# Another order at the two ends of an attention and feed-forward kernel on one core

## The reference

```
x = x + layernorm(attention(layernorm(x)))      # x: 8 sequences x 512 tokens x 256
x = x + layernorm(ffn(layernorm(x)))

attention: q, k, v = complex projections of x (16 heads x 64)
  s    = Re(rot(q) . conj(rot(k)))
  maha = max(|q|^2 + E^2 |k|^2 - 2 E s, 0) / V   # E, V: functions of |i - j|, one pair of tables per head
  logits = coef * log1p(maha / nu) - 32 * log V, causal
  y = softmax(logits) v ; output = [Re y, Im y] @ Wo
ffn: silu(x Wg^T) * (x Wu^T) @ Wd^T              # hidden 768, weights int32 / 127
```

## Time and profile before

| | us |
|---|---|
| median of 3 runs (lowest, highest) | 1871.65 (1870.67, 1872.46) |
| the profiled execution, its time | 1871.72 |
| its span | 1869.9 |
| PE busy | 1795.5 |
| DVE busy | 1631.4 |
| ACT busy | 1576.7 |
| POOL busy | 1470.0 |

### The profile page before, as it was taken

How to read it: one execution, slowest core, us unless ns; L and a number is a source line. 1 busy time by engine, 2 the same in 40 slices (tenths; PEclk the granted TensorE clock), 3 DMA queues, 4 the chain that set the end, 5 groups by cost and what they waited for, 6 DMA issues and landing times.

```text
span 1869.9 us, 35435 instructions
## 1 busy us (share of the span) xinstructions
PE 1795.5 (96%) x10690; PEld 1475.9 (79%) x10690; DVE 1631.4 (87%) x3852; ACT 1576.7 (84%) x3255; POOL 1470.0 (79%) x1291
## 2 busy tenths in 40 slices
PE   5799999999999999999999999999999999988997
PEld 3577788878888888778888888788888888867876
DVE  7799989989888899988898899888898888986885
ACT  5798888898888888998888888988888888876654
POOL 5677888878888888888888888888888888862664
PEclk9899999999999999999999999999999999999999
DMA  6311211131112201131203111120112111010111
GB/s 184 118 68 46 85 46 68 45 104 46 63 52 68 86 26 67 46 125 46 68 30 101 46 63 52 63 98 33 69 46 91 46 46 45 25 57 13 46 46 45
DMA packets 61100, 117.77 MB, mean 63 GB/s; under 512 B 13504, under 2 KB 42944, under 8 KB 52720
## 3 DMA queue, kind: packets, MB, share of 16 engines
q1 hardware_dynamic: 60528, 115.51, 18.4%
q10 hardware_dynamic: 384, 0.00, 0.0%
HBM read 99.64 MB, written 21.36 MB: 65 GB/s over the span
## 4 chain that ended last, share of the span: by engine, by line
PE 70%; DVE 11%; ACT 4%; issue 3%; POOL 2%; DMA 0%; DVEq 0%; POOLq 0%; ACTq 0%; SPq 0%
PE pa L767 15%; PE py L831 13%; PE ps L807 12%; PE po L842 10%; PE pp L797 8%; PE pp L819 6%; PE pa L778 3%; PE pa L786 2%; DVE lg L1639 2%; DVE stats L1666 1%; DVE rm L1508 1%; DVE lg L1632 1%; DVE acc L1688 1%; DVE ps L1622 1%; DVE tabs L1753 1%
## 5 line engine op out<-in xcount | busy, mean ns | idle before, releaser
L592 POOL TENSOR_TENSOR qk<-rm 64x512 f32<-64x512 f32 x504 | 697.4, 1384 | 93.7 <-PE ps L807 49.8
L602 POOL TENSOR_TENSOR ek<-tabs,kn 128x512 f32<-128x512 f32 (+3 forms) x512 | 463.7, 911 | 133.9 <-DVE lg L1632 107.0
L1639 DVE CUSTOM_DVE_ANT_0 lg<-lg,tabs,ncog 128x512 f32<-128x512 f32 (+3 forms) x512 | 445.5, 888 | 0.0
L767 PE MATMUL pa<-xt,wt 128*128 128x512 f32 x1488 | 420.8, 418 | 6.3 <-DVE rm L1514 3.7
L1508 DVE TENSOR_TENSOR rm<-pa,tabs 128x512 f32<-128x512 f32 x504 | 327.0, 676 | 75.1 <-POOL qk L592 66.1
L807 PE MATMUL ps<-qk 128*128 128x512 f32 (+3 forms) x1024 | 366.9, 443 | 12.0 <-DVE lg L1632 11.8
L831 PE MATMUL py<-pt,vt 128*128 128x128 f32 x2560 | 348.2, 275 | 0.8 <-ACT pt L1214 0.5
L1632 DVE CUSTOM_DVE_ANT_0 lg<-ps,ek,qb 128x512 f32<-128x512 f32 (+3 forms) x512 | 279.0, 545 | 76.1 <-issue 58.0
L831 PEld LDWEIGHTS py<-pt,vt 128*128 128x128 f32 x2560 | 331.1, 192 | 16.8 <-ACT pt L1214 0.7
L767 PEld LDWEIGHTS pa<-xt,wt 128*128 128x128 f32 x1488 | 273.5, 191 | 58.7 <-issue 7.9
L1199 ACT ACTIVATE lg<-lg,qb 128x512 f32<-128x512 f32 (+3 forms) x512 | 273.0, 557 | 17.4 <-DVE lg L1632 13.5
(11 more groups left out here) (205 smaller groups left out, 2251.5 us busy)
## 6 DMA issues: line engine op xcount, KB each, us to landing
xt<-xs_d SPq DMA_DIRECT2D x56, 1024.0 KB, 4.8
tabs<-vec_d SPq DMA_DIRECT2D x7, 1536.0 KB, 6.5
xs_d<-xt SPq DMA_DIRECT2D x6, 1024.0 KB, 4.3
wt<-wraw_d SPq DMA_DIRECT2D x7, 768.0 KB, 6.7
acc<-in_L_attn_x SPq DMA_DIRECT2D x8, 512.0 KB, 6.2
tabs<-in_L_attn_x SPq DMA_DIRECT2D x8, 512.0 KB, 4.8
tabs<-rope_d SPq DMA_DIRECT2D x56, 64.0 KB, 5.8
out<-tabs SPq DMA_DIRECT2D x7, 512.0 KB, 3.2
```

The source lines that it names most:

```text
L592: pool.tensor_tensor(qk[part * DH:(part + 1) * DH, z * HH + hh, :], rm[row, 2 * part, :], rm[row, 2 * part + 1, :], ALU.add if part else A ...
L602: pool.tensor_tensor(ek[:, n % 2, 0:w], tab(par, hh, E2_T, w), kn[:, hh, 0:w], ALU.mult).then_inc(ek_pool, 1)
L767: last = mm(pa[r][:, :], wproj(par, z, kt, a, r * P, (r + 1) * P), xbuf[x][:, kt, b, :], start=(n == 0), stop=(n == 3 * KT - 1))
L1639: dve.tensor_tensor_reduce(lg[:, hh, at(n)], lg[:, hh, at(n)], tab(par, hh, T3_T, w), ncog[:, par, 0, hh:hh + 1], 3e38, ALU.add, ALU.min, ...
```

## The change

SP: the wait for the last logits and decay products of the group before the last, with `f_load(0)` and `f_load(1)` behind it, moves from behind the loop into iteration 57 (group 7, second sequence). TensorE: `down` waits for five low parts, and for the sixth in front of the sixth part's first product; weight transposes 0 and 1 move into the first iteration's body; in the preparation `x_turn(1)` goes behind `first_norms_k`, with three fillers in place of two; in the last body `turn(c, 0, 1)` and `gate_up(0, 0)` go ahead of the last output product, and `gate_up(0, 1)` goes into the run-out. ScalarE: copies 0 and 1 of the weights move into the first body, and all three rounds go ahead of `log(c, 0, 2)`; three exponentials go ahead of four copies in the run-out; `x_normal(1)` goes behind the two logarithms and `x_high(1)` behind `keep_norm_k`. VectorE and GpSimd: the statistics, the move and the power of sequence 1 go further back, the statistics of sequence 2 behind V_TABLES, and the four first rotations stand together.

```diff
 SP   for t in range(G * B - 2):
             g, j = divmod(t, B)
+            if j == 1 and g == G - 1:
+                sp.wait_ge(f_dve, 8 * B * (G - 1) + 8)
+                sp.wait_ge(ek_pool, 8 * B * (G - 1) + 8)
+                f_load(0)
+                f_load(1)
...
-        sp.wait_ge(f_dve, 8 * B * (G - 1) + 8)
-        sp.wait_ge(ek_pool, 8 * B * (G - 1) + 8)
-        f_load(0)
-        f_load(1)
         for b in range(2, B):
 POOL
-        x_rstd(1)
         pool.wait_ge(w_lo, 2 * KT)
-        pool.wait_ge(x_root, 2)
         first_rotated(0, 0, 0)
         first_rotated(0, 1, 0)
+        x_rstd(1)
+        pool.wait_ge(x_root, 2)
 PE   def down(b, half):
             if half == 0:
-                pe.wait_ge(f_hl, b * FT + FT)
+                pe.wait_ge(f_hl, b * FT + FT - 1)
...
                 for r in range(FT):
+                    if half == 0 and jj == 0 and r == FT - 1:
+                        pe.wait_ge(f_hl, b * FT + FT)
 PE   body
             if it.own == 1:
+                ffn_turn(0)
+                ffn_turn(1)
                 ffn_turn(2)
...
+            if not nxt:
+                turn(c, 0, 1)
+                gate_up(0, 0)
             if old:
                 out_project(cp, it.before, 1, 1)
-            turn(c, 0, 1)
-            if nxt:
+            if nxt:
+                turn(c, 0, 1)
                 scores(cn, 0, 2)
-            else:
-                gate_up(0, 0)
-                gate_up(0, 1)
 PE   preparation
         project(c0, 0, 0, 0, 0, 0, 1, 1)
+        keep_busy(3)
+        first_norms_k()
         x_turn(c0, 1, 0)
         x_turn(c0, 1, 1)
-        keep_busy(2)
-        first_norms_k()
...
-        ffn_turn(0)
-        ffn_turn(1)
 PE   run-out
         turn(c, 1, 2)
+        gate_up(0, 1)
         attend(c, 1, 0, 1)
 ACT  body
                 square(cn, 0, 0)
+            if it.own == 1:
+                ffn_keep(0)
+                ffn_keep(1)
+                ffn_keep(2)
+                ffn_cast_of(1)
             log(c, 0, 2, it.slot)
...
-            if it.own == 1:
-                ffn_keep(2)
-                ffn_cast_of(1)
 ACT  preparation
         first_high(2)
-        x_normal(1)
         square(c0, 1, 0)
         square(c0, 1, 1)
...
-        x_high(1, 0)
-        x_high(1, 1)
+        x_normal(1)
         act.wait_ge(ncog_dve, 1)
         keep_norm_k(c0, 0, 0)
         keep_norm_k(c0, 0, 1)
+        x_high(1, 0)
+        x_high(1, 1)
...
         ffn_cast_of(0)
-        ffn_keep(0)
-        ffn_keep(1)
 ACT  run-out
         keep_turned(c, 0, 1)
+        exp(c, 1, 1)
+        exp(c, 1, 2)
+        exp(c, 1, 3)
         keep_turned(c, 0, 2)
         keep_turned(c, 0, 3)
-        exp(c, 1, 1)
         keep_turned(c, 1, 0)
-        exp(c, 1, 2)
+        keep_turned(c, 1, 1)
         keep_y(c, 0)
-        keep_turned(c, 1, 1)
-        exp(c, 1, 3)
         keep_turned(c, 1, 2)
 DVE  preparation
         angle_clamp(-1)
-        x_stats(1)
...
         first_rotate(0, RS)
+        first_rotate(0, IS)
+        first_rotate(0, IC)
         step(tt(v_e2, v_e, v_e, ALU.mult))
         step(ts(v_e, v_e, -2.0, None, ALU.mult))
-        first_rotate(0, IS)
-        first_rotate(0, IC)
-        x_move(1)
+        x_stats(1)
         first_rotate(1, RC)
...
         first_rotate(1, IC)
+        x_move(1)
         start(0, 0)
-        x_stats(2)
...
         assert done[0] == V_TABLES, done
+        x_stats(2)
```

More of the change, by code:

```diff
@@ L485, in refill, with f_load @@
                 load_decay(g, par)
+            def f_load(b):
+                sp.dma_start(f_xin[b % 2], x_d[b].rearrange("(j p) n -> p j n", p=P)).then_inc(f_x[b % 2], 16)
             for t in range(G * B - 2):
@@ L517, in _ @@
                     load_rope(g + 1, (g + 1) % 2)
-            def f_load(b):
-                sp.dma_start(f_xin[b % 2], x_d[b].rearrange("(j p) n -> p j n", p=P)).then_inc(f_x[b % 2], 16)
             def f_store(b):
```

## The result

| | before | after |
|---|---|---|
| median, us | 1871.7 (20 runs, 1868.95 to 1873.21) | 1868.0 (20 runs, 1867.07 to 1869.32) |
| the profiled execution, its time and span | 1871.72, 1869.9 | 1869.32, 1867.5 |

The ratio after to before is 0.9982, 95% interval 0.9976 to 0.9989: 3.7 us faster, where 6.3 were forecast. The profiled executions differ by 2.4 us; the one of after is the slowest of its 20 runs.

A forecast was written before the change was run, and what follows sets the result against it. TensorE was taken to bound the long middle (396.8 of 400 us), so time could be won only outside it. Gains of 3.8 + 0.2 + 0.1 + 2.2 = 6.3 us from 1871.7 gave 1865.4 us, range 1862.3 to 1868.8.

The forecast's parts named there:

- rival C: Preparation gains nothing net, from low clock and weight turns in the first iteration's path; 1867.6, up to 1868.5 us; chance 0.17.
- the two signs that I had named for being wrong: Forecast wrong if the feed-forward's period falls by over 0.3 us, or the middle's first value product doesn't come earlier.
- rival E: Third iteration from the end: VectorE's own operations hold TensorE nearly as long; loads give 1.0, total 1868.5 us; chance 0.06.
- Part 1, loads: Third iteration from the end: earlier residual loads win 2.5 us idle time and 1.3 low clock, 3.8; least 2.5, most 4.3.
- That iteration at 26 to 26.6 us: Third iteration from the end, 30.02 us before, was to take 26 to 26.6 us once the loads came early.
- Part 2, sixth part: Feed-forward: the 1.01 us idle before down moves one product on, the period stays; gain 0.2 us, bounds 0 and 5.3.
- The ring over ScalarE's normalization and silu: Feed-forward: VectorE's loop through ScalarE's normalization, copy and silu sets the 18.94 us period, with no matmul late in it.
- Part 3, run-out: Run-out: 0.5 us lost and 0.6 won up to out_project(0,0), chain behind unchanged; gain 0.1 us, bounds +1.3 and -1.6.
- Part 4, preparation: Preparation: 0.9 us won up to the first weight cast, 1.7 behind it, less for clock; 2.2 us, bounds 4.5 and -6.6.
- The clock, which I weighed at 0.4: Preparation: TensorE's clock may fall in the longer gap, costing some 1 us; the gain was taken as 2.2, not 2.6.
- first_norms_k 1 to 1.6 us earlier: Preparation: the norm products, at 33.45 before, were to start 1 to 1.6 us earlier.
- the second square near 50.5: Preparation: the second square, at 53.07 before, was to come near 50.5.

The follow-up runs named there:

- e5: Kernel after with ScalarE's silu(b, 2) moved ahead of f_normal(b + 1): 1868.50 us, ratio to before 0.9989.
- e3: Kernel before with only the new order of the run-out: 1871.17 us, ratio to before 0.9995.
- e10: Kernel after with the first down bank evicted earlier and VectorE's hidden(b, 0) ahead of second_norm(b + 1): 1873.54 us, ratio to before 1.0015.
- e12: Kernel after with the edits of e5, e9 and e10, and five table steps ahead of GpSimd's first rotation: 1869.14 us, ratio to before 0.9986.
- e4: Kernel before with only the new order of the preparation: 1871.86 us, ratio to before 0.9998.
- e7: Kernel after with keep_busy(8) instead of keep_busy(3) ahead of first_norms_k: 1868.50 us, ratio to before 0.9989.
- e1: Kernel before with only the early loads of the residual input: 1869.91 us, ratio to before 0.9988.
- e11: Kernel before with both edits of e10, down still waiting for all six parts: 1878.20 us, ratio to before 1.0038.
- e9: Kernel after with ScalarE's eviction of the first down bank ahead of hidden_high(b, 5): 1869.17 us, ratio to before 0.9986.

## Why the prediction was right, and where it was not

The sign and the range held, and the mechanism of the largest term; the gain forecast was 2.6 us too large. That the range held is owed to its width. 1868.0 lies outside the forecast's own range (1863 to 1867.4) and in that of rival C, at 0.17. Of the two signs that I had named for being wrong, the period of the feed-forward didn't fall, but the first value product did not come earlier either: 68.15 against 67.78. Two sums were slightly off: rival E gives 1868.2, not 1868.5, and 7.1 - 5.5 is 1.6, not 1.7.

- **Part 1, loads: 3.8 predicted, 2.6 measured.** The wait went, residual_sum slowed down to 2.88 us (2.68 expected) and ended 8.8 us into the iteration, where I had it at 8.6. Two terms were mis-sized. TensorE's waits in the iteration fell from 2.98 to 1.2 us and not to 0.5: behind the wait of 0.57 stand three smaller ones (0.20, 0.15, 0.32), all for VectorE, which is busy for 26.08 of the 27.43 us and so, as I read it, doesn't catch up. And the low clock had cost 0.8 us, TensorE's busy time from 27.00 to 26.16, not 1.3. 1.8 + 0.8 = 2.6, at the lower bound that I had set. "That iteration at 26 to 26.6 us" was wrong by 0.8. The 26.09 us that I called one iteration of the middle is the one with the first layer norm; between most other neighbours in the middle of the trace there are 25.1.
- **Part 2, sixth part: 0.2 predicted, about 0.5 measured.** The period stayed at 18.9 and the idle time moved one product on, as predicted. Half of it stopped earlier, at down's own bank (0.47), which I had not seen. The gain lies at the first down product: from value product 63 to it 37.87 us in e5 and 38.30 in e3 (old wait), 0.4; and 0.1 in the last sequence. The reason that I gave was half of it. The ring over ScalarE's normalization and silu is there (e10, e12), and no matmul is late in it. What it lacked is the second ring of the same length, over gate_up's second half and the transposes (e5), which keeps the period where it is when the first is opened. In the old kernel hidden(b,0) ended only 0.2 us ahead of the product that needs it (1748.64 and 1748.84 in the earlier trace rows), so this second ring was all but closed beside the wait that was removed.
- **Part 3, run-out: 0.1 predicted, 0.2 measured** (e3: 38.30 against 38.53 in before). The low clock that cost the profiled run 1.6 us comes and goes between executions, with either order.
- **Part 4, preparation: 2.2 predicted, 0.3 to 0.7 measured (e4, after), and one piece of it, 0.5, clear of chance.** In the pair of profiles 0.37 us were lost up to the first value product, 0.70 won by the shorter low clock in the first iterations, 0.49 won between iterations 3 and 4 and 0.13 lost behind them. This is the step that failed, and with it "first_norms_k 1 to 1.6 us earlier" (0.85 later) and "the second square near 50.5" (54.78). I had written that two table operations run beside GpSimd's rotations "and lose up to 0.8". Four did, and lost 0.80 + 0.97 + 0.83 + 0.89 = 3.5 us, in a stretch where VectorE is busy for 1.9 of every 2 us. The clock, which I weighed at 0.4, cost nothing at the end (e7). Rival C had the total right (1867.6 to 1868.5), but blamed the clock and the weight turns and not the contention, and it kept part 1 at 3.8. The miss has two halves: part 1 was 1.2 too large and the preparation 1.5.

The sum of what was measured: 2.6 + 0.5 + 0.2 + 0.7 = 4.0, less 1.6 for the clock in the run-out, makes the 2.4 us between the profiled executions. That the medians differ by more, 3.7, fits a clock that falls in some executions only; which of the timed ones had it isn't recorded, so this stays open. The run-out is not the only such place: in last_down the clock fell in 12 of the 14 profiles, before and after among them, and stayed in e1 and e11. From sequence 6's down product to the end e1 takes 29.8 us and before 31.3, 1.5 us that none of the terms above holds.

The Trainium skill (SBUF — State Buffer, Who interferes with whom) says that a VectorE operation with two inputs in SBUF, or a one-input copy or scalar operation in its fast mode, and a GpSimd operation that reads SBUF hold each other off for a whole instruction, and that operations outside these classes don't. The traces agree: 0.16 to 1.25 us for a two-input operation of four columns begun 0.06 us behind a GpSimd operation of 1.29; 0.48 to 1.45 for a scalar step; and 1.39 to 1.41 us for the statistics of one input, with or without GpSimd.

## What to carry to other kernels

When a step is moved on VectorE, look at what GpSimd does at its new place: short operations on two operands, or scalar steps in SBUF, cost up to one GpSimd operation each there, and ahead of GpSimd's first operation they are cheap. A wait that disappears is a gain only if no second chain of nearly the same length closes over it: add up both rings from the rows before pricing it. And compare the gain with what the same code differs by between two profiles (here 1.4 us at iteration 60), before a term of that size is counted, and look in both for stretches of low clock: setting them apart told here what the totals could not.

## What was not expected of the hardware

- The same instruction stream reached iteration 60 between 1606.53 and 1607.94 us in four profiles that differ only behind it (after, e5, e9, e10); by iteration 3 the two short ones were already 1.4 us or more ahead of the two long ones (90.31 and 90.39 us against 91.79 and 91.84), the granted clock being 0.97 or more against 0.50 in the stretch from 88 to 90.
- The granted clock fell to 0.50 in thin stretches of the run-out in 5 of 14 profiles, once with the run-out unchanged, with TensorE busy about 1.0 of each 2 us in the four microseconds ahead whether it fell or not, and in just those profiles whose low clock in iteration 0 had been short. What ties the two places is not known.
- Fillers that kept the clock up to the norm products (e7) saved 1.8 us in them, and the first value product came 0.04 us earlier.
